# Flamingo block with gated experts and a modulated MLP: two Q/K buffers, six projection products a head, weights split on GpSimd, first up product over six heads

## The chip, the cores and the metric

The kernel runs on one core of one Trainium2 chip. The metric is the device time of one execution in microseconds (us). Three runs of the kernel before took 1077.31, 1077.67 and 1080.08 us; their median is 1077.67 us.

The engines are called by the profile's short names: PE is TensorE (matmuls and transposes), DVE is VectorE, ACT is ScalarE, POOL is GpSimd, SP is SyncE, which here only issues DMAs.

## The reference, cut to what matters

There are 4 batches of 512 tokens with 512 features. First comes a layer norm and an expert layer, in which each token uses one of four experts. Then, on the layer-normed result, a transformer block whose attention output is used only through a 16-wide factor:

```
x1 = x + tanh(g_xattn) * expert_layer(layernorm(x))
y  = layernorm(x1)
h1 = rmsnorm(y) * ln1_w ;  h = rmsnorm(y) * ln2_w
q, k, v = h1 @ Wq.T, h1 @ Wk.T, h1 @ Wv.T          # 16 heads of 32
probs = softmax(causal(q k^T / sqrt(32)))          # per head
attn  = (probs @ v) @ Wo.T
mod   = 0.1 * tanh(attn @ A)                       # 16 wide
gate  = silu(h @ W_in.T + mod * (h @ A) @ B)       # 2048 wide
up    = h @ W_up.T
out   = x1 + tanh(g_ffn) * (y + (gate * up) @ W_down.T)
```

All of it is float32. The kernel gets this precision by writing each operand of a matmul as a high part (rounded by a copy) and a low part (the rest, found by a subtraction), and by three matmuls in the place of one: high times high, low times high, high times low. So a product with a contraction over 512 features is 4 x 3 = 12 matmuls ("12 products"); half of it is 6.

## The kernel before, in words

The expert layer is worked off in 19 items of 128 token rows (the first 160 us of the trace). Then follow the four batches, one after the other; each has a short prelude, the attention over 16 heads, and the MLP in 16 chunks of 128 hidden features. Each engine runs its own instruction stream in order; a semaphore wait in a stream holds up everything behind it in that stream.

The 16 heads of a batch are four quads (`q` = 0 to 3) of four heads (`j` = 0 to 3). Q and K of a quad are one 128-row tile each: the product of the projection weights `wqs` and the transposed rows `hT`, in PSUM bank `QKB` (3). ACT copies the product into its high part (`split_qk`), DVE subtracts to get the low part (`qk_low`, the helper line L1326), and SP copies each head's 32 rows into the buffer `stack` (L307). `qk` holds one quad.

The heads are pipelined. In the step of head n (`head_step`), each engine does this, in this order:

- PE: part of a projection product if the step has one (L510); the transposes of head n+1's probabilities (`turn_probs`, L709; 10 of them), the first of which waits for the first low part of head n, since it overwrites the bank that this is read from; the scores of head n+3 (`scores`, L681 and L685); the product with the values of head n (`attend`, L722; 8 matmuls), which waits for all three low parts of head n.
- ACT: the exponentials of head n+1 (L962) and part of their scaling (L969); `split_qk` where the step has one; the three high parts of head n's turned probabilities (L878).
- DVE: reciprocals and scaling for head n+1 (L1343, L1347); `qk_low` where the step has one; the four row maxima of head n+2 (`maxima`, L1338); the three low parts of head n's turned probabilities (L1326).
- POOL: its part of the scaling (L485), and the low part of a later quad's projection weights (L474).

In the kernel before, K of quad q+1 is projected whole (12 products) at the start of the step j=0 of quad q, and Q of quad q+2 in halves at the start of j=2 and j=3; quads 2 and 3 have less or none of it. ACT's `split_qk` and DVE's `qk_low` take Q of quad q+1 in the step j=0 of quad q, and K of quad q+1 in j=1. So each of them comes one step after the step in which PE finished the product. The high part of the weights is one ACT copy per quad after j=1. Quads 0 and 1 are a hardware loop.

The last quad fills the steps with the first chunk's up product: 3, 3 and 6 products in j = 0, 1, 2 (`up_part`, L769).

The prelude projects Q and K of quad 0 (banks 6 and 7) and Q of quad 1, makes the values (banks 4 and 7), turns the first probabilities, and then clears bank 7 (`ATT`) by a matmul with zeros before the first step.

Of the kernel before, what the change touches and what calls it, by code (L numbers as in the profile page):

```python
# [12 lines left out]
P = 128  # L13
# [27 lines left out]
FIRST_QK = (6, 7)  # L41
VALUES, LOW_RANK = (4, 7), 5
# [12 lines left out]
NORM_AT = 4  # L55

# [3 lines left out]
def build(nc, x, ids, wexp, wov, amat, bmat, ln, gates, wqk, wmlp, out):  # L60
    ctx = ExitStack()
    with ctx:
# [31 lines left out]
        qk = carve(6144, 2048).rearrange("p (m t) -> p m t", m=4)  # L94
        pts = carve(8192, 4 * PACKED).rearrange("p (h a c) -> p h a c", h=2, a=2)
        VS = QH * 64 + 64
        vst = carve(8192 + 4 * PACKED, TT * VS).rearrange("p (t c) -> p t c", t=TT)
        vst_v = vst[:, :, 0:QH * 64].rearrange("p t (h c) -> p t h c", h=QH)
# [155 lines left out]
        def _(sp):  # L254
# [39 lines left out]
            def load_stack(b, q, j):  # L294
                g = b * NQ + q
                if j == 0:


                    sp.wait_ge(qk_lo, g * 2 + 2)
                elif type(q) is int and j == 1:  # L300
                    pass
                else:

                    sp.wait_ge(s_done, g * (3 * QH) + (j - 1) * 3)
                rows = slice(HD * j, HD * j + HD)
                for k, (a, c) in enumerate(((Q_HI, K_HI), (Q_LO, K_HI), (Q_HI, K_LO))):
                    sp.dma_start(stack[HD * k:HD * k + HD, j % 2, :, :].bitcast(F32),  # L307
                                 qk[rows, a:c + 1:c - a, :].bitcast(F32)).then_inc(stk[j % 2], 16)
# [33 lines left out]
            def batch(b, more, first=False):  # L342
                for j in range(2):
                    load_stack(b, 0, j)
                if not first:
                    store_before(b)
                for j in range(2, QH):
                    load_stack(b, 0, j)
                if not first:
                    load_residual(b)  # L350
                with sp.Fori(1, NQ) as q:
# [38 lines left out]
        def _(pool):  # L390
# [26 lines left out]

            def gather(i):
# [47 lines left out]
            for i in range(5 + DT, ITEMS):  # L466
                turn(i)
                if i == ITEMS - 4:
                    pool.wait_ge(wq_hi, 1)
                    g.tensor_tensor(wqs[:, LO, :, :, :], wqk_v[:, :, :, 0:P], wqs[:, HI, :, :, :].bitcast(F32),  # L470
                                    ALU.subtract).then_inc(wq_lo, 1)

            def low(dst, src, high, done):
                g.tensor_tensor(dst, src, high.bitcast(F32), ALU.subtract).then_inc(done, 1)  # L474

            def weights_low(b, q):
                src = wqk_v[:, :, :, bass.ds(q * P, P)]
                pool.wait_ge(wq_hi, b * NQ + q + 1)
                low(wqs[:, LO, :, :, :], src, wqs[:, HI, :, :, :], wq_lo)
# [7 lines left out]
            for b in range(NB):  # L487

                weights_low(b, 1)
                normalise(b * H)  # L490
                for q in range(NQ):
                    for j in range(QH):
                        if q < NQ - 1 or j < QH - 1:
                            normalise((b * NQ + q) * QH + j + 1)
                        if j == 1 and q < NQ - 2:
                            weights_low(b, q + 2)
                if b < NB - 1:

                    weights_low(b + 1, 0)
# [3 lines left out]
        def _(pe):  # L503
# [149 lines left out]
            def project(b, q, which, to=QKB, half=None):  # L653
# [44 lines left out]
            def turn_probs(n, par, first=False):  # L698
# [27 lines left out]
            def head_step(b, q, j, ahead):  # L726
# [12 lines left out]
                if not ahead and j < QH - 1:  # L739
                    if j == 0:  # L740
# [4 lines left out]
                    up_part(0, ((0,), (1,), (2, 3))[j])  # L745
                if ahead or j < QH - 3:
# [18 lines left out]
            def up_part(par, tiles):  # L765

                for k in tiles:
                    for i, (pl, pr) in enumerate(PARTS):
                        mm = pe.matmul(bank[UP[par]][:, :], wch[:, par, pl, (DT + k) * P:(DT + k) * P + P],  # L769
                                       hT[:, pr, k, :], start=k == 0 and i == 0, stop=k == DT - 1 and i == len(PARTS) - 1,  # L770
                                       skip_group_check=True)
                if DT - 1 in tiles:
# [28 lines left out]
            def batch(b, more):  # L801
# [7 lines left out]
                for k in range(DT):  # L809
                    for part in (HI, LO):  # L810
# [3 lines left out]
                values((0, 1))  # L814

# [8 lines left out]
                turn_probs(b * H, 0, first=True)  # L824
                scores(b * H + 2, 0, b * (H // 2) * 48 + 96)

                pe.wait_ge(vpb_ok, b + 1)
                pe.matmul(bank[ATT][:, :], zeror[:, :], hT[:, HI, 0, :], start=True, stop=False,
                          skip_group_check=True).then_inc(pv_done, 1)
                with pe.Fori(0, NQ - 2) as q:  # L830
                    for j in range(QH):
                        head_step(b, q, j, 2)
                for q, ahead in ((NQ - 2, 1), (NQ - 1, 0)):
                    for j in range(QH):
                        head_step(b, q, j, ahead)
# [38 lines left out]
        def _(act):  # L874
# [68 lines left out]
            def split_wqk(b, q):  # L943

                copy(wqs[:, HI, :, :, :], wqk_v[:, :, :, bass.ds(q * P, P)]).then_inc(wq_hi, 1)

            def split_qk(b, q, which, first=False, at=QKB):
                n = b * NQ + q
                act.wait_ge(qk_done, n * 2 + which + 1)
                if which == 0 and not first:  # L950

                    for k in range(2):
                        act.wait_ge(stk[k], n * 96)
                copy(qk[:, (Q_HI, K_HI)[which], :], bank[at][:, :]).then_inc(qk_hi, 1)
# [16 lines left out]
            def head_step(b, q, j, ahead):  # L971
                n = (b * NQ + q) * QH + j
                if ahead or j < QH - 1:
# [8 lines left out]
                if j == 0:  # L982
# [5 lines left out]
                    copy(vst_v[:, :, :, 0:R], vp[:, :, bass.ds(q * QH, QH), :]).then_inc(vst_hi, 1)  # L988

            def quad(b, q, ahead):  # L990
                for j in range(QH):
                    head_step(b, q, j, ahead)
                    if j == 1 and ahead == 2:
                        split_wqk(b, q + 2)
# [36 lines left out]
            def batch(b, more):  # L1031
                split_qk(b, 0, 0, True, FIRST_QK[0])
                split_gate_up(b, 0, 0)
                split_qk(b, 0, 1, True, FIRST_QK[1])
# [15 lines left out]
                with act.Fori(0, NQ - 2) as q:  # L1050
                    quad(b, q, 2)
                quad(b, NQ - 2, 1)
                for j in range(QH):
                    head_step(b, NQ - 1, j, 0)
# [82 lines left out]
        def _(dve):  # L1137
# [190 lines left out]
            def qk_low(b, q, which, at=QKB):  # L1328
                dve.wait_ge(qk_hi, (b * NQ + q) * 2 + which + 1)
                low(qk[:, (Q_LO, K_LO)[which], :], bank[at][:, :], qk[:, (Q_HI, K_HI)[which], :], qk_lo)  # L1330
# [18 lines left out]
            def head_step(b, q, j, ahead):  # L1349

                one_more, two_more = ahead or j < QH - 1, ahead or j < QH - 2
# [3 lines left out]
                if j < 2 and ahead:  # L1355
                    qk_low(b, q + 1, j)
# [5 lines left out]
                if j == 0:  # L1362
                    dve.wait_ge(vst_hi, b * NQ + q + 1)
                    low(vst_v[:, :, :, 32:32 + R], vp[:, :, bass.ds(q * QH, QH), :], vst_v[:, :, :, 0:R], vst_lo)

            def quad(b, q, ahead):


                for j in range(QH):
                    head_step(b, q, j, ahead)  # L1370
# [90 lines left out]
            def batch(b, more):  # L1461
# [7 lines left out]
                normalise(b * H, 0)  # L1469
                maxima(b * H + 1)  # L1470
# [3 lines left out]
                with dve.Fori(0, NQ - 2) as q:  # L1474
                    quad(b, q, 2)
                quad(b, NQ - 2, 1)
                quad(b, NQ - 1, 0)
# [161 lines left out]
```

## Time and profile before

| | |
|---|---|
| median of three runs | 1077.67 us |
| profiled execution, time | 1080.39 us |
| profiled execution, span | 1078.7 us |
| mean granted TensorE clock | 0.997 of 2.4 GHz |
| PE busy | 1035.0 us (96%) |
| DVE busy | 735.5 us (68%) |
| ACT busy | 613.1 us (57%) |
| POOL busy | 177.7 us (16%) |
| steps and prelude of batch 1 | 390.6 to 485.1 us of the span |
| its MLP | 485.1 to about 619 us |

The profile comes from one execution. The profiled execution is 2.7 us above the median of the three runs. Busy time on PE is modelled with the matmuls' drains, so neighbouring matmuls overlap; the distance from one start to the next is what an instruction costs its stream. The views used below are the page itself, the busy time by stretch, the waits, the timeline of one engine (start, duration, engine, line, what it writes and reads, and in brackets the idle time ahead of it with what ended it), and the chain that ended last.

### The profile page before, as it was taken

The numbers are of one execution on the slowest core, as the hardware profiler recorded it, in microseconds if no ns is written. First come the engines' busy times: TensorE is split into PE (matmuls) and PEld (weight loads), VectorE is DVE, ScalarE is ACT, GpSimd is POOL, SyncE is SP. The second block draws the span as 40 slices with busy tenths as digits, with TensorE's granted clock in tenths as the row PEclk, the third lists the DMA queues.
The fourth block names the chain that finished last, engine by engine and source line by source line (L and its number), as shares of the span: only waits on it lengthen the run. The fifth ranks groups of instructions, "written<-read, shape, count | busy, mean of one in ns | idle before, by whom it ended". The sixth has DMA issues, their size and how long they took to land.

```text
span 1078.7 us, 17949 instructions
## 1 busy us (share of the span) xinstructions
PE 1035.0 (96%) x5336; PEld 860.9 (80%) x5337; DVE 735.5 (68%) x1662; ACT 613.1 (57%) x1463; POOL 177.7 (16%) x156
## 2 busy tenths in 40 slices
PE   6999999999999999989999999999999999899998
PEld 6787878777888888878888888778888877788887
DVE  7766747996665559985664589966655689854443
ACT  4464547886444458875444378864354588754342
POOL 4536122320000003320000024200000133200000
PEclk9899999999999999999999999999999999999999
DMA  6534132443322425243322354432234342333221
GB/s 244 188 141 165 39 118 70 97 100 120 105 88 90 151 69 140 64 119 128 108 89 88 108 142 97 112 117 88 88 102 141 85 121 68 79 91 105 88 88 49
DMA packets 47063, 115.59 MB, mean 107 GB/s; under 512 B 6800, under 2 KB 6800, under 8 KB 46096
## 3 DMA queue, kind: packets, MB, share of 16 engines
q1 hardware_dynamic: 43968, 105.06, 33.1%
q0 software_dynamic: 3040, 9.96, 2.7%
q14 instruction: 40, 0.33, 0.1%
q8 instruction: 15, 0.25, 0.1%
HBM read 76.46 MB, written 13.37 MB: 83 GB/s over the span
## 4 chain that ended last, share of the span: by engine, by line
PE 80%; DVE 9%; issue 3%; DMA 3%; ACT 2%; SPq 1%; POOL 1%; DVEq 0%; ACTq 0%; POOLq 0%
PE bank L510 64%; PE bank L709 4%; PE bank L722 3%; DVE wr L1326 3%; DVE nb L1338 3%; PE bank L681 3%; DMA stack<-wr 2%; PE bank L758 1%; SPq L307 1%; DVE big L1347 1%; PE bank L685 1%; ACT big L962 1%; PE bank L769 1%; PE bank L566 1%; DMA big<-in_x,gidx 1%
## 5 line engine op out<-in xcount | busy, mean ns | idle before, releaser
L510 PE MATMUL bank<-hT,wr 128*128 128x512 f32 x1488 | 358.4, 390 | 0.0
L510 PEld LDWEIGHTS bank<-hT,wr 128*128 128x128 f32 x1488 | 278.9, 188 | 59.9 <-issue 1.3
L510 PE MATMUL bank<-wr,actr 128*128 128x512 f32 (+1 forms) x1224 | 303.3, 397 | 2.2 <-DVE actr L1308 1.5
L510 PEld LDWEIGHTS bank<-wr,actr 128*128 128x128 f32 x1224 | 229.1, 190 | 51.1 <-issue 3.3
L1376 DVE SCALAR_TENSOR_TENSOR wr<-stream,lns,wr 128x256 fp32r<-128x256 f32 x256 | 122.3, 538 | 51.0 <-ACT wr L1001 51.0
L1326 DVE TENSOR_TENSOR wr<-bank,wr 128x512 fp32r<-128x512 f32 (+1 forms) x224 | 124.6, 600 | 19.7 <-ACT wr L878 19.7
L962 ACT ACTIVATE big<-bank,nb 128x512 f32<-128x512 f32 (+3 forms) x256 | 131.7, 531 | 9.7 <-DVE nb L1338 8.2
L878 ACT ACTIVATE actr<-act_sb 128x512 fp32r<-128x512 f32 x64 | 40.4, 632 | 145.7 <-DVE act_sb L1390 145.7
L878 ACT ACTIVATE wr<-bank 128x512 fp32r<-128x512 f32 (+1 forms) x224 | 102.6, 532 | 27.8 <-PE bank L510 18.7
L1013 ACT ACTIVATE sil<-bank 128x512 f32<-128x512 f32 x64 | 38.1, 596 | 137.6 <-PE bank L758 137.6
L485 POOL TENSOR_SCALAR big<-big,rr 128x256 f32<-128x256 f32 x64 | 78.0, 1219 | 205.9 <-DVE rr L1343 205.9
L474 POOL TENSOR_TENSOR wqs<-wstage,wqs 128x1024 fp32r<-128x1024 f32 x15 | 36.2, 2410 | 453.4 <-ACT wqs L878 453.4
L1001 ACT ACTIVATE wr<-stream,lns 128x256 fp32r<-128x256 f32 x256 | 108.4, 494 | 0.0
L1338 DVE TENSOR_REDUCE nb<-bank 128x1 f32<-128x512 f32 (+3 forms) x256 | 107.0, 476 | 1.3 <-PE bank L685 1.0
L709 PE MATMUL bank<-ident,big 128*128 128x128 f32 x640 | 86.0, 277 | 22.2 <-DVE wr L1326 22.2
L709 PEld LDWEIGHTS bank<-ident,big 128*128 128x128 f32 x640 | 70.6, 140 | 34.6 <-DVE wr L1326 25.6
L510 PE MATMUL bank<-hT,wqs 128*128 128x512 f32 x384 | 96.3, 398 | 0.9 <-DVE wr L1326 0.9
L1326 DVE TENSOR_TENSOR wr<-stream,wr 128x512 fp32r<-128x512 f32 x64 | 43.8, 690 | 72.4 <-ACT wr L878 71.7
L722 PE MATMUL bank<-wr 128*64 128x512 f32 (+3 forms) x512 | 84.2, 307 | 0.0
L1390 DVE TENSOR_TENSOR act_sb<-bank,sil 128x512 f32<-128x512 f32 x64 | 44.2, 691 | 58.3 <-PE bank L510 51.5
L510 PEld LDWEIGHTS bank<-hT,wqs 128*128 128x128 f32 x384 | 69.7, 188 | 15.8 <-DVE wr L1326 2.2
L722 PEld LDWEIGHTS bank<-wr 128*64 128x64 f32 x512 | 62.0, 134 | 18.8
(182 smaller groups left out, 1078.6 us busy)
## 6 DMA issues: line engine op xcount, KB each, us to landing
stream<-in_wmlp SPq DMA_DIRECT2D x64, 512.0 KB, 4.0
stack<-wr SPq DMA_DIRECT2D x192, 128.0 KB, 2.3
stream<-in_wmlp SPq DMA_DIRECT2D x64, 256.0 KB, 2.7
big<-in_x SPq DMA_DIRECT2D x4, 1024.0 KB, 5.5
big<-y_rows SPq DMA_DIRECT2D x4, 1024.0 KB, 5.6
residual<-big SPq DMA_DIRECT2D x4, 1024.0 KB, 5.1
big<-residual SPq DMA_DIRECT2D x4, 1024.0 KB, 5.6
out<-big SPq DMA_DIRECT2D x3, 1024.0 KB, 4.5
```

What stands on the lines that cost most here:

```text
L485: g.tensor_scalar(rows, rows, rr[:, n % 2, qt:qt + 1], None, ALU.mult).then_inc(pn_pool, 1)
L510: mm = pe.matmul(dst, lhs(pl, k), rhs(pr, k), start=start and i == 0, stop=stop and i == n - 1, skip_group_check=skip)
L709: mm = pe.transpose(bank[bk][:, col + (qt - kt) * P:col + (qt - kt) * P + P], prob[par][:, src:src + P], ident[:, :])
L722: mm = pe.matmul(bank[ATT][0:64, kt * P:S], vst[:, kt, 64 * j:64 * j + 64], pts[:, j % 2, part, at:at + w], start=False, stop=False, skip_ ...
L878: return a.activation(dst, src, ACT.Copy)
L962: a.activation(prob[par][:, at:at + w], bank[bk][:, col:col + w], ACT.Exp, bias=nb[:, qt:qt + 1], accum_out=rs[:, par, qt:qt + 1]).then_in ...
L1001: ins = a.activation(dst[:, :, dt, :], raw[:, :, dt, :], ACT.Copy, scale=lns[:, 1, dt:dt + 1])
L1013: a.activation(sil[:, :], bank[GATE[par]][:, :], ACT.Silu).then_inc(g_silu, 1)
L1326: v.tensor_tensor(dst, src, high.bitcast(F32), ALU.subtract).then_inc(done, 1)
L1338: v.reduce_max(nb[:, qt:qt + 1], bank[bk][:, col:col + P * (qt + 1)], AXX, negate=True).then_inc(nb_ok, 1)
L1376: ins = v.scalar_tensor_tensor(out=dst[:, :, dt, :], in0=raw[:, :, dt, :], scalar=lns[:, 1, dt:dt + 1], in1=high[:, :, dt, :].bitcast(F32) ...
L1390: v.tensor_tensor(act_sb[:, :], bank[UP[par]][:, :], sil[:, :], ALU.mult).then_inc(gu_ok, 1)
```

## The change

What it does:

- `qk` has two buffers, one for even and one for odd quads. ACT waits for `stack` loads of the quad two before instead of the one before.
- PE's projections are in halves of 6 products: K of quad 1 half in the prelude and half at the start of step 0; then one half at the start of every step of quads 0 and 1 (K of q+1 second half in j=0; Q of q+2 in j=1 and j=2; K of q+2 first half in j=3); in quad 2 only j=0 has one.
- ACT's `split_qk` and DVE's `qk_low` take K of quad q+1 in j=0 and Q of quad q+2 in j=2. Q of quad 1 is taken in the prelude.
- The high part of the projection weights of quads 2 and 3 moves from ACT to POOL, and the weights are split for Q and K apart.
- The first up product goes in 6 parts of 2 products into the steps of heads 9 to 14.
- K of quad 0 uses bank 3, the second half of the values bank 6, and the clearing of bank 7 comes before the first scores; the wait for the values' copy moves into `turn_probs`, ahead of its last two transposes.
- The loops over quads are written out; `vst` loses 64 unused columns.

```diff
-FIRST_QK = (6, 7)
-VALUES, LOW_RANK = (4, 7), 5
+FIRST_QK = (6, 3)
+VALUES, LOW_RANK = (4, 6), 5
+UP_PARTS = 6
+UP_FROM = H - 1 - UP_PARTS
@@ GpSimd
+            def weights_high(b, q, which):
+                pool.wait_ge(qk_done, (b * NQ + q - 1) * 2 + which + 1)
+                g.tensor_copy(wqs[:, HI, which, :, :], wqk_v[:, which, :, q * P:q * P + P]).then_inc(wq_hi, 1)
...
-                        if j == 1 and q < NQ - 2:
-                            weights_low(b, q + 2)
+                        if j < 2 and q < NQ - 2:
+                            weights_high(b, q + 2, j)
+                            weights_low(b, q + 2, j)
@@ TensorE: project, turn_probs, head_step
-                    pe.wait_ge(wq_hi, n + 1)
-                    pe.wait_ge(wq_lo, n + 1)
-                    if which and to == QKB:
-                        pe.wait_ge(qk_lo, n * 2 + 1)
+                    pe.wait_ge(wq_lo, n * 2 + which + 1)
+                    if q:
+                        pe.wait_ge(qk_lo, n * 2 + which)
...
+                    elif first and kt == 2:
+                        pe.wait_ge(vpb_ok, values_out)
...
-                if j == 2 and ahead == 2:
-                    project(b, q + 2, 0, half=0)
-                if j == 0 and ahead:
-                    project(b, q + 1, 1)
-                if j == 3 and ahead == 2:
-                    project(b, q + 2, 0, half=1)
-                if ahead or j < QH - 1:
+                if j == 0 and q < NQ - 1:
+                    project(b, q + 1, 1, half=1)
+                elif j and q < NQ - 2:
+                    project(b, q + 2, (0, 0, 1)[j - 1], half=(0, 1, 0)[j - 1])
+                if head < H - 1:
                     turn_probs(n + 1, (j + 1) % 2)
...
-                    up_part(0, ((0,), (1,), (2, 3))[j])
+                    up_part(0, head - UP_FROM)
@@ TensorE: batch
-                with pe.Fori(0, NQ - 2) as q:
+                project(b, 1, 1, half=0)
+                for q in range(NQ):
...
@@ ScalarE head_step
-                if j < 2 and ahead:
-                    split_qk(b, q + 1, j)
+                if j == 0 and q < NQ - 1:
+                    split_qk(b, q + 1, 1)
+                elif j == 2 and q < NQ - 2:
+                    split_qk(b, q + 2, 0)
@@ VectorE head_step
                 if one_more:
                     normalise(n + 1, (j + 1) % 2)
-                if j < 2 and ahead:
-                    qk_low(b, q + 1, j)
+                if j == 0 and q < NQ - 1:
+                    qk_low(b, q + 1, 1)
+                elif j == 2 and q < NQ - 2:
+                    qk_low(b, q + 2, 0)
                 if two_more:
                     maxima(n + 2)
```

## Rows read from the trace of the kernel before

**Rows 1.** The page: busy time of each engine, and TensorE's granted clock in 40 slices.

```profile
PE 1035.0 (96%) x5336; PEld 860.9 (80%) x5337; DVE 735.5 (68%) x1662; ACT 613.1 (57%) x1463; POOL 177.7 (16%) x156
PEclk9899999999999999999999999999999999999999
```

**Rows 2.** Busy time by stretch: batch 0's MLP, batch 1's heads (clock, DMA share, GB/s last).

```profile
256.00:390.00 134.00, 134.00 (x601) 110.52 (x600) 74.60 (x161) 58.82 (x116) 2.54 (x1) 1.00 0.33 107
410.00:486.00 76.00, 70.14 (x455) 58.09 (x454) 70.52 (x161) 63.74 (x190) 22.93 (x17) 1.00 0.39 102
```

**Rows 3.** Waits of PE, whole span: total us, times, longest.

```profile
PE bank L709 <- DVE wr L1326: 22.2, 28, 1.2
```

**Rows 4.** Timeline of PE: a step with a half projection, batch 1.

```profile
447.35 1.60 PE L510 MATMUL bank<-hT,wqs 128*128 128x512 f32 x6
448.79 1.25 PE L709 MATMUL bank<-ident,big 128*128 128x128 f32 x10
449.80 0.47 PE L681 MATMUL bank<-stack 96*128 96x512 f32 x1
...
450.82 1.33 PE L722 MATMUL bank<-wr 128*64 128x512 f32 x8
451.99 3.00 PE L510 MATMUL bank<-hT,wqs 128*128 128x512 f32 x12
```

**Rows 5.** Timeline of PE, batch 1: transposes that open each step's work, and the end.

```profile
408.90 1.25 PE L709 MATMUL bank<-ident,big 128*128 128x128 f32 x10
...
414.47 1.26 PE L709 MATMUL bank<-ident,big 128*128 128x128 f32 x10
...
458.79 1.47 PE L709 MATMUL bank<-ident,big 128*128 128x128 f32 x10 [0.59 <-DVE wr L1326]
...
463.23 1.47 PE L709 MATMUL bank<-ident,big 128*128 128x128 f32 x10 [0.55 <-DVE wr L1326]
464.45 0.48 PE L681 MATMUL bank<-stack 96*128 96x512 f32 x1
...
467.50 1.47 PE L709 MATMUL bank<-ident,big 128*128 128x128 f32 x10 [0.69 <-DVE wr L1326]
...
477.09 1.47 PE L709 MATMUL bank<-ident,big 128*128 128x128 f32 x10 [1.06 <-DVE wr L1326]
...
485.06 5.69 PE L510 MATMUL bank<-hT,wr 128*128 128x512 f32 x24
```

**Rows 6.** Timeline of DVE, batch 1: the values' low part, and one whole step.

```profile
454.38 0.41 DVE L1326 TENSOR_TENSOR wr<-big,wr 128x256 fp32r<-128x256 f32 x1
...
464.02 0.16 DVE L1343 RECIPROCAL rr<-rs 128x4 f32<-128x4 f32 x1
464.22 1.04 DVE L1347 TENSOR_SCALAR big<-big,rr 128x512 f32<-128x512 f32 x2
465.18 1.67 DVE L1338 TENSOR_REDUCE nb<-bank 128x1 f32<-128x512 f32 x4
466.77 1.60 DVE L1326 TENSOR_TENSOR wr<-bank,wr 128x512 fp32r<-128x512 f32 x3
```

**Rows 7.** Chain that ended last, batch 1's prelude: product, high part, low part of K.

```profile
387.96 8.22 PE bank L510 x36
396.20 0.61 ACT wr L878
396.83 0.70 DVE wr L1326
```

**Rows 8.** Groups by line, shapes apart: POOL's weight splits.

```profile
L474 POOL TENSOR_TENSOR wqs<-wstage,wqs 128x1024 fp32r<-128x1024 f32 x15 | 36.2, 2410 | 453.4 <-ACT wqs L878 453.4
```

**Rows 9.** Busy time by stretch, early in the expert stage.

```profile
30.00:40.00 10.00, 8.02 (x30) 6.08 (x30) 7.61 (x21) 3.19 (x5) 5.99 (x9) 0.73 0.79 249
40.00:50.00 10.00, 10.00 (x48) 8.23 (x47) 7.65 (x24) 5.88 (x8) 3.58 (x4) 0.92 0.16 52
```

**Rows 10.** Timeline of PE: one product of 12 in that stretch.

```profile
37.24 4.97 PE L510 MATMUL bank<-wr,actr 128*128 128x512 f32 x12 [0.34 <-DVE actr L1299]
```

More of the change, by code:

```diff
@@ L299, in load_stack @@
                     sp.wait_ge(qk_lo, g * 2 + 2)
[L300 removed]
+                elif q == 0 and j == 1:
                     pass
@@ L350, in batch @@
                     load_residual(b)
-                with sp.Fori(1, NQ) as q:
+                for q in range(1, NQ):
                     for j in range(QH):
@@ L468, in _ @@
                 if i == ITEMS - 4:
[L469 to L479, printed above, removed]
+                    for which in range(2):
+                        weights_low(0, 0, which)
             def normalise(n):
@@ L487, in _ @@
             for b in range(NB):
-                weights_low(b, 1)
+                for which in range(2):
+                    weights_low(b, 1, which)
                 normalise(b * H)
@@ L744, in head_step @@
                         pe.wait_ge(cg_lo, b * NCH + 1)
-                    up_part(0, ((0,), (1,), (2, 3))[j])
-                if ahead or j < QH - 3:
+                    up_part(0, head - UP_FROM)
+                if head < H - 3:
                     m = b * (H // 2) + q * 2 + (j + 3) // 2
@@ L763, in up_product, with up_part @@
                               lambda p, k: hT[:, p, k, :], DT).then_inc(u_done, 1)
[L765 to L772, printed above, removed]
+            def up_part(par, part):
+                n = DT * len(PARTS) // UP_PARTS
+                for i in range(part * n, part * n + n):
+                    k, (pl, pr) = i // len(PARTS), PARTS[i % len(PARTS)]
+                    mm = pe.matmul(bank[UP[par]][:, :], wch[:, par, pl, (DT + k) * P:(DT + k) * P + P],
+                                   hT[:, pr, k, :], start=i == 0, stop=i == DT * len(PARTS) - 1,
+                                   skip_group_check=True)
+                if part == UP_PARTS - 1:
                     mm.then_inc(u_done, 1)
@@ L814, in batch @@
                 values((0, 1))
+                pe.matmul(bank[ATT][:, :], zeror[:, :], hT[:, HI, 0, :], start=True, stop=False,
+                          skip_group_check=True).then_inc(pv_done, 1)
                 pe.wait_ge(qk_lo, b * (NQ * 2) + 2)
@@ L823, in batch @@
                 pe.wait_ge(ha_ok, b + 1)
-                turn_probs(b * H, 0, first=True)
+                turn_probs(b * H, 0, first=True, values_out=b + 1)
                 scores(b * H + 2, 0, b * (H // 2) * 48 + 96)
-                pe.wait_ge(vpb_ok, b + 1)
-                pe.matmul(bank[ATT][:, :], zeror[:, :], hT[:, HI, 0, :], start=True, stop=False,
-                          skip_group_check=True).then_inc(pv_done, 1)
-                with pe.Fori(0, NQ - 2) as q:
+                project(b, 1, 1, half=0)
+                for q in range(NQ):
                     for j in range(QH):
[L832 to L835, printed above, removed]
+                        head_step(b, q, j)
                 pe.wait_ge(exp_ok, (b + 1) * H * 4)
@@ L943, in split_wqk, with split_qk @@
             def split_wqk(b, q):
-                copy(wqs[:, HI, :, :, :], wqk_v[:, :, :, bass.ds(q * P, P)]).then_inc(wq_hi, 1)
-            def split_qk(b, q, which, first=False, at=QKB):
+                for which in range(2):
+                    copy(wqs[:, HI, which, :, :], wqk_v[:, which, :, q * P:q * P + P]).then_inc(wq_hi, 1)
+            def split_qk(b, q, which, at=QKB):
                 n = b * NQ + q
                 act.wait_ge(qk_done, n * 2 + which + 1)
-                if which == 0 and not first:
+                if which == 0 and q >= 2:
                     for k in range(2):
-                        act.wait_ge(stk[k], n * 96)
-                copy(qk[:, (Q_HI, K_HI)[which], :], bank[at][:, :]).then_inc(qk_hi, 1)
+                        act.wait_ge(stk[k], (n - 1) * 96)
+                copy(qk[:, q % 2, (Q_HI, K_HI)[which], :], bank[at][:, :]).then_inc(qk_hi, 1)
             def exponentials(n, par):
@@ L987, in head_step @@
                     act.wait_ge(vst_zero, 1)
[L988 to L994, printed above, removed]
+                    copy(vst_v[:, :, :, 0:R], vp[:, :, q * QH:q * QH + QH, :]).then_inc(vst_hi, 1)
             def split_gate_up(b, c, par):
@@ L1049, in batch @@
                 normalise(b * H, 0)
[L1050 to L1054, printed above, removed]
+                split_qk(b, 1, 0)
+                for q in range(NQ):
+                    for j in range(QH):
+                        head_step(b, q, j)
                 for par in range(2):
@@ L1363, in head_step @@
                     dve.wait_ge(vst_hi, b * NQ + q + 1)
[L1364 to L1370, printed above, removed]
+                    low(vst_v[:, :, :, 32:32 + R], vp[:, :, q * QH:q * QH + QH, :], vst_v[:, :, :, 0:R], vst_lo)
             def gate_up_low(b, c, par):
@@ L1469, in batch @@
                 normalise(b * H, 0)
+                qk_low(b, 1, 0)
                 maxima(b * H + 1)
@@ L1473, in batch @@
                               bank[VALUES[1]][:, :]).then_inc(vpb_ok, 1)
[L1474 to L1477, printed above, removed]
+                for q in range(NQ):
+                    for j in range(QH):
+                        head_step(b, q, j)
                 for par in range(2):
```

42 lines of the change are left out of this document (24 added, 18 removed).

## The prediction

> **What bounds the kernel now.** I read the page first. PE is busy 96% of the span, DVE 68%, and the granted clock stands at nine tenths or more in every slice [rows 1]. So PE is where time is, but a share over the whole span does not say what a stage is worth, so the busy time by stretch came next. In the MLP of a batch PE is busy 134.00 of 134.00 us; nothing of this change touches that stage, and only less PE work could shorten it. In the heads of a batch PE is busy 70.14 of 76.00 us and DVE 70.52 of 76.00 [rows 2]: two engines are both nearly full and hand work to each other. The waits say which hand-over ends late: PE's transposes wait for DVE's low parts, 22.2 us in 28 waits, the longest 1.2 us [rows 3]. That is the whole prize: some 5.5 us a batch.
>
> The timelines show how a step is made up. PE, when it never waits: half a projection 1.44 us (447.35 to 448.79), transposes 1.01, scores 1.02, product with the values 1.17 (450.82 to 451.99), 4.64 us together [rows 4]. Without the projection it is 3.20, and then PE waits: from one step to the next there are 4.27 us (463.23 to 467.50), and the transposes after a wait take 1.22 us to the next start rather than 1.01 [rows 5]. DVE's step is the same 4.27: reciprocal and scaling 1.16 (464.02 to 465.18), maxima 1.59 (to 466.77), low parts 1.53 busy of which the first ends just ahead of the transposes at 467.50, 0.73 us after the low parts began [rows 5, 6]. So steps with half a projection are bound by PE (4.64) and empty ones by DVE (4.27), and spreading the projections evenly looks right. What counts is what DVE's queue waits for in each step.
>
> **The change part by part.**
>
> *The new hand-over.* In the changed code the half that completes a product stands at the start of a step (j=0 for K, j=2 for Q), and in this same step ACT's high part and DVE's low part of it stand ahead of work that PE needs at once. DVE's order is scaling, `qk_low`, maxima, low parts of head n. PE's next instruction after the half projection is the transposes of head n+1, whose first waits for the first low part of head n. Before, the product was a step old when DVE came to it; now it isn't finished when DVE arrives. PE therefore finishes the half, and stands still until ACT and DVE have gone through everything between. Queued behind DVE's wait are the four maxima and the three low parts, behind ACT's the three high parts; PE waits for both.
>
> The price, from rows: start of the half to its last result 1.60 us (the six matmuls' busy time) [rows 4]; ACT starts at 396.20, 0.02 after the product's end at 387.96 + 8.22, and DVE 0.63 after that; the low part 0.70, of which 0.1 overlaps the next, so 0.60 [rows 7]; maxima 1.59 [rows 6]; first low part and hand-over 0.73 [rows 5, 6]. Sum 1.60 + 0.02 + 0.63 + 0.60 + 1.59 + 0.73 = 5.17 us from the start of the half to the transposes, where it was 1.44 without a wait. PE stands idle for 3.57 us of it.
> This comes in j=0 of quads 0, 1, 2 and j=2 of quads 0, 1: 5 times a batch, 20 in all. The bounds of one: below, 3.2 us idle, if DVE's pieces follow each other as closely as in [rows 6] and the hand-overs cost nothing; above, 4.0, by 0.1 more at each of four hand-overs.
>
> *Period of the steps.* With such a hand-over: 1.01 + 1.02 + 1.17 + 5.17 = 8.37 us (transposes to transposes; the ones that open it did not wait) [rows 4]. The step after it has an ordinary half, and its opening transposes did wait: 1.22 + 1.02 + 1.17 + 1.44 = 4.85 [rows 4, 5]. DVE needs 4.27, in j=0 another 0.34 for the values' low part (0.41 less overlap) [rows 6], so 4.61: hidden under PE's 4.85.
>
> *One batch*, in the times of batch 1, by the start of the transposes of head n, T(n). T(0) = 408.90 stays [rows 5]. Then PE does 1.01 + 1.02 + 1.44, and up to 0.5 us for the values' copy, which the last two transposes now wait for (eight transposes and DVE's copy both begin when the values end); I take 0.3. The completing half starts at 412.67, T(1) = 412.67 + 5.17 = 417.84, against 414.47. The zeros' matmul no longer stands there; it falls in PE's wait for the first `stack` load.
> T(9) = 417.84 + 4 x (8.37 + 4.85) = 470.72. The step to T(10) is DVE's, 4.27 + 0.34, so 475.33, against 458.79: 16.5 us late.
> T(10) to T(14) was 18.30 [rows 5]. Now an up part of two products (1.44 / 3 = 0.48 us) stands between transposes and scores in each of four steps, where before one of three products did. Behind the scores stand DVE's maxima; DVE has some 0.3 us of slack there, so each of two steps gives 0.15, and in the quad's first step, where the exponentials are late anyhow, 0.48: in all 18.30 + 0.8 = 19.1. T(14) = 494.4.
> From T(14) to the MLP it was 7.97 [rows 5], all PE or nearly. Four products (0.96 us) less stand there now: 7.0. The MLP begins at 501.4, against 485.06: 16.4 us later, of which the five idle spells are 17.9, their slower restart 1.0, and the evened steps give some 2.5 back.
>
> *POOL's new work.* The low part of 1024 columns takes 2.41 us [rows 8], for half of them some 1.2. The high copy on POOL isn't in the trace; it lies between nothing and 2.41, I take 1.2, as a subtraction of the same size. It is needed by a half projection at least a step later, after 8.37 us, with POOL busy 22.93 of 76 us in this stage [rows 2]. It costs nothing; without that cover it would be up to 2.4 us per quad. ACT gets its copy's time back, but ACT isn't what PE waits for.
>
> *The second buffer, the banks, the written-out loops.* ACT's wait for `stack` loads is behind PE's idle spells: nothing. The splits in the expert stage and in the MLP lie beside a PE that is busy all the time: nothing. For written-out loops I take nothing, within 1 us a batch either way.
>
> *Sum.* 4 x 16.4 = 65.6 us on the profiled execution's 1080.39 gives 1146. The median of the runs is 2.7 us lower: 1077.67 + 65.6 = 1143.3. The bounds: 20 spells by -0.4 and +0.4 give 8 either way, the rest 4: **1131 to 1156**, at an unchanged clock.
>
> **The rivals.**
>
> *The clock falls in the spells.* PE idles 3.6 us in each 13.2 us of the first nine steps; no wait of the transposes before is longer than 1.2 [rows 3]. Early in the expert stage there is a fall to the lower level, 1.2 GHz: a mean of 0.73 over 10 us and 0.92 over the next is 5.4 and 1.6 us at half clock, 7.0 together [rows 9], after short bursts with gaps between. In it 12 products with their restart took 4.97 us [rows 10], against 3.00 at 2.4 GHz [rows 4]. If each spell brought such a fall, 7.0 us would do the work of 4.2, so 2.8 us more each, 20 x 2.8 = 56: 1143 + 56 = 1199. If a third did, 1162. For it: the spells are three times as long as any there now. Against: between two of them lie 9.6 us of dense work. The Trainium skill, "TensorE: Matmul & The Clock Gate", section "HAM oscillation — how this bites in real kernels", warns of just such waits of a few microseconds between bursts, after which every burst starts slow. By that rule this rival's 1199 would be the time; no row here has a spell this long in a dense stretch.
>
> *Shorter spells.* PE's half ends earlier for DVE than its modelled busy end says, and the hand-overs overlap more than in the rows: at half of the maxima's time, 0.8 us a spell, 20 x 0.8 less, 1127. Against it: the hand-overs of [rows 7] are the same kinds of instructions.
>
> *Faster.* The completed products are always there when DVE comes, as before. Then the eight steps from T(1) to T(9) take PE's 4.64, with DVE at 4.27 and at most 0.6 + 0.34 more in a step: 37.1 to 38 us, the next 4.6; T(10) comes at 414.1 + 42.4 = 456.5, 2.3 us earlier, the end 2.5 earlier: 10 in all, 1068. It holds if PE runs at least one step ahead of DVE. Against it: PE cannot, since its transposes wait for the low part that stands behind `qk_low` in DVE's queue. If a second quad's work were taken from a product a step old, this would decide; in the diff it is not.
>
> *The change does nothing*, if the program were bound elsewhere in these steps: PE and DVE are both over 92% busy there [rows 2], so a wait added to both must show.
>
> **How the numbers follow.** Forecast (spells at full clock) 0.72; clock falls 0.16; shorter spells 0.06; faster 0.04; nothing 0.02. Predicted 1143 us. Below 1124 lie the last two and some of the shorter spells; above 1185 lies the half of the clock's rival with a fall in nearly every spell. So 1124 to 1185. A difference under 0.3% (3 us) can't be told from none. Faster 0.04, same 0.02, slower 0.94.
>
> **What would show it.** On PE five waits of some 3.6 us a batch ahead of L709's transposes, ended by DVE's low parts, 20 in all and some 71 us together; on DVE a wait of about 3 us for ACT's high part of K or Q, on ACT one for PE's product, in steps 0, 2, 4, 6, 8; steps alternating between 8.4 and 4.9 us; the clock's row still at 9. The first up product in six pieces, with no wait over 1 us. The MLP stays at its time to the microsecond. It is wrong if the waits are there but the clock's row is lower, or if the steps come out even at 4.6 to 4.9 us with no wait for the product.

## The result and the profile after

The changed kernel takes 1184.73 us (median of 4 runs, 1183.39 to 1185.4) against 1078.88 us of the kernel before in the same session: ratio 1.098, 95% interval 1.0956 to 1.1002. The profiled execution took 1183.39 us, its span 1181.3. The page after, its first rows and the granted clock ([rows 1] before):

```profile
PE 1074.6 (91%) x5336; PEld 892.5 (76%) x5337; DVE 738.6 (63%) x1662; ACT 609.7 (52%) x1463; POOL 191.4 (16%) x188
PEclk9999998899999998899999998899999988899999
```

PE has 40 us more busy time for the same 5336 instructions, so some ran slower, and the clock's row dips four times: once in each batch's heads. The busy time by stretch says the same (heads of batch 1, then its MLP and the first 5 us of the next prelude; after the us of each engine come clock, DMA share and GB/s; [rows 2] before). The MLP keeps a clock of 1.00 and its length; the 0.8 us without work in its row are two gaps ahead of the next batch's first products:

```profile
420.00:540.00 120.00, 98.07 (x565) 82.44 (x564) 85.36 (x188) 75.96 (x221) 29.75 (x26) 0.90 0.36 98
540.00:675.00 135.00, 134.18 (x596) 109.99 (x596) 75.99 (x164) 57.35 (x117) 2.89 (x2) 1.00 0.30 93
```

The wait of the transposes for DVE, 22.2 us before [rows 3], is now

```profile
PE bank L715 <- DVE wr L1324: 86.9, 39, 4.0
```

and PE's timeline shows what a batch looks like (batch 1, only the transposes that open each step's work, [rows 5] before; the product between is shown once):

```profile
441.99 2.14 PE L715 MATMUL bank<-ident,big 128*128 128x128 f32 x10 [3.60 <-DVE wr L1324]
...
448.32 1.25 PE L715 MATMUL bank<-ident,big 128*128 128x128 f32 x10
...
451.52 1.61 PE L515 MATMUL bank<-hT,wqs 128*128 128x512 f32 x6
457.17 2.39 PE L715 MATMUL bank<-ident,big 128*128 128x128 f32 x10 [4.03 <-DVE wr L1324]
...
464.51 1.25 PE L715 MATMUL bank<-ident,big 128*128 128x128 f32 x10
...
472.93 2.25 PE L715 MATMUL bank<-ident,big 128*128 128x128 f32 x10 [3.60 <-DVE wr L1324]
```

A spell every second step, 3.6 to 4.0 us long, where 3.57 was forecast. DVE at the second of them ([rows 6] before):

```profile
454.23 0.69 DVE L1324 TENSOR_TENSOR wr<-bank,wr 128x512 fp32r<-128x512 f32 x1 [4.92 <-ACT wr L880]
454.84 1.67 DVE L1336 TENSOR_REDUCE nb<-bank 128x1 f32<-128x512 f32 x4
456.43 1.61 DVE L1324 TENSOR_TENSOR wr<-bank,wr 128x512 fp32r<-128x512 f32 x3
```

At 454.23 DVE has idled 4.92 us for ACT's high part of Q. It then runs low part, maxima, first low part in the order in which they are queued, and PE's transposes start at 457.17, 0.74 us after the low parts began.

What the forecast left out is in the same transposes: 2.14 to 2.39 us for what takes 1.47 after a wait [rows 5]. The busy time of PE by the microsecond (PE busy, clock, DMA share, GB/s), from the spell on:

```profile
455.00:456.00 1.00, 0.00 (x0) 1.00 0.00 0
456.00:457.00 1.00, 0.00 (x0) 0.53 0.00 0
457.00:458.00 1.00, 0.83 (x4) 0.50 0.00 0
...
461.00:462.00 1.00, 1.00 (x5) 0.50 0.00 0
462.00:463.00 1.00, 1.00 (x6) 0.55 0.55 127
463.00:464.00 1.00, 1.00 (x7) 1.00 0.77 180
```

In this spell the clock falls to 1.2 GHz (0.50) while PE idles and comes back after 5.7 us of work; transposes, scores and the product with the values take 5.90 us (457.17 to 463.07) where they took 3.4. This is one of the dearer falls. Behind the batch's first spell PE starts again at 441.99; the clock falls some 0.4 us after that and is back within 4 us:

```profile
442.00:443.00 1.00, 1.00 (x6) 0.71 0.79 182
...
445.00:446.00 1.00, 1.00 (x7) 0.59 0.00 0
```

Gone through by the microsecond, the whole trace shows a fall at 19 of the 20 spells. The one without, at 188 us, was 3.60 us long like others that had one. The low stretches of the 19 come to 95.5 us, 5.0 us each on average.

### The profile page after: what moved, and what is told of

The parts are those of the page before. It is cut to its first block, busy times and chain, and to the rows that moved or that the text cites. A ratio compares the mean times of both kernels' runs of the same rounds, so it can differ in the third digit from the quotient of the medians.

```text
span 1181.3 us, 17663 instructions
## 1 busy us (share of the span) xinstructions
PE 1074.6 (91%) x5336; PEld 892.5 (76%) x5337; DVE 738.6 (63%) x1662; ACT 609.7 (52%) x1463; POOL 191.4 (16%) x188
## 4 chain that ended last, share of the span: by engine, by line
PE 82%; DVE 8%; issue 3%; ACT 3%; DMA 2%; SPq 1%; DVEq 0%; POOL 0%; ACTq 0%; POOLq 0%
PE bank L515 60%; PE bank L715 8%; PE bank L728 5%; PE bank L684 4%; DVE nb L1336 4%; DVE wr L1324 3%; DMA stack<-wr 2%; PE bank L688 2%; ACT wr L880 2%; PE bank L763 1%; PE bank L571 1%; SPq L309 1%; PE bank L586 1%; PE bank L775 1%; ACT big L965 1%
## 5 line engine op out<-in xcount | busy, mean ns | idle before, releaser
L715 PE MATMUL bank<-ident,big 128*128 128x128 f32 x640 | 104.9, 318 | 86.9 <-DVE wr L1324 86.9
L715 PEld LDWEIGHTS bank<-ident,big 128*128 128x128 f32 x640 | 85.0, 162 | 104.7 <-DVE wr L1324 77.0
L427 POOL TENSOR_TENSOR wqs<-wstage,wqs 128x512 fp32r<-128x512 f32 x32 | 42.7, 1346 | 437.2 <-ACT wqs L880 435.8
L728 PE MATMUL bank<-wr 128*64 128x512 f32 (+3 forms) x512 | 92.5, 326 | 0.3
L728 PEld LDWEIGHTS bank<-wr 128*64 128x64 f32 x512 | 67.6, 146 | 22.4 <-issue 3.9
L684 PE MATMUL bank<-stack 96*128 96x512 f32 (+3 forms) x256 | 83.1, 393 | 1.0 <-DMA stack<-wr 0.5
```

The lines of the kernel that those rows point to most:

```text
L427: g.tensor_tensor(wqs[:, LO, which, :, :], wqk_v[:, which, :, q * P:q * P + P], wqs[:, HI, which, :, :].bitcast(F32), ALU.subtract).then_i ...
L684: pe.matmul(bank[bk][:, col:col + w], stack[:, par, 0, qt * P:qt * P + P], stack[:, par, 1, 0:w], start=start, stop=False, skip_group_chec ...
L715: mm = pe.transpose(bank[bk][:, col + (qt - kt) * P:col + (qt - kt) * P + P], prob[par][:, src:src + P], ident[:, :])
L728: mm = pe.matmul(bank[ATT][0:64, kt * P:S], vst[:, kt, 64 * j:64 * j + 64], pts[:, j % 2, part, at:at + w], start=False, stop=False, skip_ ...
```

## The experiments

Twelve kernels ran, each beside the kernel before on the same chip; ratios are to it. The texts put on record ahead of each run call the explanations by letters. Theory A: PE stands still behind the product's own low part, and the clock falls because PE stands still.

**e1: the parts at the end of the step.** In ACT and DVE the call moves behind the loop over the three parts of head n:

```diff
 DVE head_step (ACT likewise with split_qk, copy)
-                if j == 0 and q < NQ - 1:
-                    qk_low(b, q + 1, 1)
-                elif j == 2 and q < NQ - 2:
-                    qk_low(b, q + 2, 0)
...
                     low(pts[:, j % 2, LO, at:at + w], ...)
+                if j == 0 and q < NQ - 1:
+                    qk_low(b, q + 1, 1)
+                elif j == 2 and q < NQ - 2:
+                    qk_low(b, q + 2, 0)
```

> Changed kernel, but in the steps that complete a product ACT makes its high part after the three high parts of head n, and DVE its low part after the three low parts of head n, instead of ahead of them. Product positions on PE, both Q/K buffers, POOL's splits and the six up parts stay. Theory A (PE stands still because its transposes wait behind the product's own low part, and the clock falls from that): the 20 waits of 3.6 to 4.0 us vanish, no wait over 1.5 us is left, granted clock back to 0.99 or more, steps 1 to 8 of a batch 37 to 38 us, time about 1070. Rival B (POOL's splits, the two buffers or the longer program cost the time): the waits stay and the time stays above 1120. Rival C (the low part is now too late for the stack load of the next quad): waits of PE's scores for the DMA of about 1 us, three a batch, time about 1082.

Measured: 1127.64 us (1.0449, 1.0431 to 1.0466), mean clock 0.977, a fall at 14 of the 20 products. The waits for the low parts went (longest 1.1 us), but another took their place:

```profile
PE bank L684 <- ACT big L965: 37.6, 20, 2.0
PE bank L715 <- DVE wr L1324: 13.2, 18, 1.1
```

Twenty waits again, one a product. ACT now waits for the product at the end of its step, and queued behind that are the next head's exponentials, for which PE's scores wait since they overwrite the bank. ACT's timeline shows the queue:

```profile
424.53 0.60 ACT L880 ACTIVATE wr<-bank 128x512 fp32r<-128x512 f32 x1 [2.35 <-PE bank L515]
425.03 0.41 ACT L880 ACTIVATE wr<-big 128x256 fp32r<-128x256 f32 x1
425.33 0.68 ACT L965 ACTIVATE big<-bank,nb 128x512 f32<-128x512 f32 x1
```

Neither A, which saw no second queue and said 1070, nor B or C foretold this. The DVE part of the chain is confirmed; ACT's part had been overlooked.

**e2: maxima first.** One exchange on DVE, ACT as it was:

```diff
-                if j == 0 and q < NQ - 1:
-                    qk_low(b, q + 1, 1)
-                elif j == 2 and q < NQ - 2:
-                    qk_low(b, q + 2, 0)
                 if two_more:
                     maxima(n + 2)
+                if j == 0 and q < NQ - 1:
+                    qk_low(b, q + 1, 1)
+                elif j == 2 and q < NQ - 2:
+                    qk_low(b, q + 2, 0)
```

> Changed kernel, with one pair of DVE calls exchanged: the four maxima of head n+2 before the product's low part instead of behind it. ACT and PE unchanged. Theory A: the maxima (1.59 us) leave the chain from product to transposes, so each of the 20 waits goes from 3.6 to 2.0 us. With the clock no longer falling: 32 us for the waits and some 35 us for the clock, 1118. With the clock falling as before: about 1153. Rival (the wait is not this chain): no change, 1185.

Measured: 1159.16 us (1.075, 1.0709 to 1.0791), clock 0.966. The spells fell by the maxima's time, to 2.01 to 2.44 us:

```profile
PE bank L715 <- DVE wr L1324: 54.9, 38, 2.4
PE bank L684 <- ACT big L965: 6.8, 12, 0.9
```

86.9 - 54.9 = 32.0 us off the transposes' waits, the 32 forecast; 6.8 came back as waits for exponentials. The case with a falling clock (1153) is the nearer one: the clock fell at 14 of the 20 spells, though each was only 2.0 to 2.4 us long.

**e3: the spells filled.** Fourteen matmuls with zero weights where PE stood still:

```diff
                 elif j and q < NQ - 2:
                     project(b, q + 2, (0, 0, 1)[j - 1], half=(0, 1, 0)[j - 1])
+                if (j == 0 and q < NQ - 1) or (j == 2 and q < NQ - 2):
+                    for _ in range(14):
+                        pe.matmul(bank[ATT][:, :], zeror[:, :], hT[:, HI, 0, :], start=False, stop=False,
+                                  skip_group_check=True)
```

> Changed kernel with 14 more matmuls (512 columns, zero weights, added into the values' bank, which they leave as it is) on PE right behind each half that completes a product, where PE now stands idle; nothing else is changed. They take 14 x 0.22 = 3.1 us of the 3.6. Theory A (the chain sets the step, and the clock's part of the loss comes from PE being idle): the step's length by the chain stays, the clock stays at 2.4 GHz, and the time falls by the clock's part alone, some 35 to 40 us, to about 1147, although PE does 280 more matmuls. Rival D (the slow matmuls behind the waits have another cause than idle time): clock row as low as before and time 1185 or more. Rival E (PE is the bound): 62 us more, 1245.

Measured: 1150.37 us (1.0668, 1.065 to 1.0686), clock 0.999. PE does 280 matmuls more, 3.3 us a spell, and the kernel is 34.4 us faster:

```profile
431.65 3.33 PE L744 MATMUL bank<-hT,zeror 128*128 128x512 f32 x14
435.41 1.47 PE L715 MATMUL bank<-ident,big 128*128 128x128 f32 x10 [0.43 <-DVE wr L1328]
```

The transposes are back at 1.47 us, and still the last thing that they wait for is DVE's low part, so the fill did not lengthen the chain. The clock's part is thus 34.4 us, 1.7 a spell; PE as the bound (E) and another cause for the slow matmuls (D) fall.

**e4: the places of before.** All of the change but the steps of products and parts:

```diff
-                if j == 0 and q < NQ - 1:
-                    project(b, q + 1, 1, half=1)
-                elif j and q < NQ - 2:
-                    project(b, q + 2, (0, 0, 1)[j - 1], half=(0, 1, 0)[j - 1])
+                if j == 2 and q < NQ - 2:
+                    project(b, q + 2, 0, half=0)
+                if j == 0 and q < NQ - 1:
+                    project(b, q + 1, 1)
+                if j == 3 and q < NQ - 2:
+                    project(b, q + 2, 0, half=1)
... DVE (ACT likewise with split_qk)
-                if j == 0 and q < NQ - 1:
-                    qk_low(b, q + 1, 1)
-                elif j == 2 and q < NQ - 2:
-                    qk_low(b, q + 2, 0)
+                if j < 2 and q < NQ - 1:
+                    qk_low(b, q + 1, j)
```

> Changed kernel with the projections and their high and low parts put back where they were (K of the next quad whole in j=0, Q of the quad after in halves in j=2 and j=3; parts in j=0 and j=1, one step after the product), in PE, ACT and DVE. Two buffers, POOL's high and low splits, the banks, written-out loops and the six up parts stay. Theory A: those parts cost nearly nothing; 1076 to 1082. Rival B (these parts cost the time): above 1120.

Measured: 1081.21 us (1.0019, 1.0003 to 1.0036). POOL's splits, the second buffer, the banks, the written-out loops and the six up parts together cost about 2 us (0.3 to 3.9 by the interval). Rival B falls.

**e5 and e6: a product a step old, from either side.** e5 moves PE's halves one step earlier (with them POOL's splits, and K of quad 1 is whole in the prelude) and leaves ACT's and DVE's parts; e6 leaves PE and moves the parts.

```diff
 e5, PE
-                if j == 0 and q < NQ - 1:
-                    project(b, q + 1, 1, half=1)
-                elif j and q < NQ - 2:
-                    project(b, q + 2, (0, 0, 1)[j - 1], half=(0, 1, 0)[j - 1])
+                if q < NQ - 2:
+                    project(b, q + 2, j // 2, half=j % 2)
 e6, DVE (ACT likewise with split_qk)
-                if j == 0 and q < NQ - 1:
+                if j == 1 and q < NQ - 1:
                     qk_low(b, q + 1, 1)
-                elif j == 2 and q < NQ - 2:
+                elif j == 3 and q < NQ - 2:
                     qk_low(b, q + 2, 0)
```

> Changed kernel with PE's half projections one step earlier: K of quad 1 whole in the prelude, then Q of quad q+2 in j=0 and j=1 and K of quad q+2 in j=2 and j=3 of quads 0 and 1. ACT's and DVE's parts stay in j=0 and j=2, so each product is a step old when they come, as in the kernel before. POOL splits the weights a step earlier too, and SP's load for a quad's first head also waits for the scores of the head two before. Theory A (a product must be a step old): no wait of PE above 1.2 us, clock 0.99 or more, steps 1 to 7 at 4.65 us, time 1070 to 1082. Rival F (both parts in one step with the maxima overload DVE or ACT, whatever the age of the product): waits of 1 to 2 us stay in the steps 0, 2, 4, 6, 8 and the time above 1110.

> Changed kernel with PE as it is, and ACT's high and DVE's low part of K moved from j=0 to j=1, those of Q from j=2 to j=3, at the same place within the step (after the scaling, ahead of the maxima). The product is then a step old from the other side. Theory A: no wait of 1.8 us or more for exponentials (as the late order within the step had) or low parts. Left over: the scores of the next quad's first head wait for its stack load, since K's low part comes 2.7 us after the transposes and SP and the DMA take 4.1 us more, about 1 us, three times a batch: 1080 to 1090, clock 0.99. Rival F: above 1110.

Measured: e5 1089.73 us (1.0103, 1.0088 to 1.0119), clock 0.998; e6 1079.80 us (1.0009, 1.0 to 1.0019), clock 0.997. Both lose the spells, and the slow clock but for one fall in e6. With six products in each of the first nine steps of e6, PE waits 19.0 us for low parts:

```profile
PE bank L715 <- DVE wr L1324: 19.0, 23, 1.7
```

Of the DMA waits expected for e6, about 1 us three times a batch, next to nothing is there:

```profile
PE bank L684 <- DMA stack<-wr: 1.0, 3, 0.5
```

e5 is 8 us over the top of A's range: its projection of Q of quad 2 now waits in step 0 for DVE to free the bank (row below, 6.0 us in all), and it has eight steps without a projection, where e6 has seven. The rest of e5's excess I haven't traced.

```profile
PE bank L521 <- DVE wr L1328: 6.0, 4, 1.5
```

**e7 and e8: is DVE's load what bounds the empty steps?** One line, in e5's kernel (e7) and in the kernel before (e8):

```diff
-NORM_DVE, NORM_ACT, NORM_POOL = (3, 2), (0,), (1,)
+NORM_DVE, NORM_ACT, NORM_POOL = (3,), (2,), (1, 0)
```

> The kernel with halves one step earlier, and the probabilities' scaling spread anew: DVE scales only the 512 columns of tile 3, ACT tile 2 (384) and POOL tiles 1 and 0 (256 and 128). DVE's step falls from 4.27 to some 3.8 us, ACT's rises by 0.1, POOL's by 0.6. Theory A with DVE as the bound of the empty steps: the seven steps without a projection shorten by some 0.3 each, 8 to 14 us in all below the kernel with halves earlier. Rival G (in the empty steps the chain scores, maxima, low part, transposes is the bound, not DVE's load): under 3 us below it.

> Kernel before, with only the scaling spread anew (DVE tile 3, ACT tile 2, POOL tiles 1 and 0). It has seven steps a batch bound by DVE at 4.27 us and PE needs 3.2 us in them: 4 x 7 x 0.3 to 0.45 = 8 to 13 us less, about 1067. Rival G: within 3 us of the kernel before.

Measured: e7 1087.32 us, 2.4 below e5; e8 1080.07 us (1.0012, 1.0 to 1.0025). DVE's busy time fell by 30 us; e7 gained 2.4 us by it and e8 nothing. Both are inside what rival G gave (under 3 us), and outside the 8 to 14 us of the other case. DVE in an empty step of e8:

```profile
464.78 0.49 DVE L1347 TENSOR_SCALAR big<-big,rr 128x512 f32<-128x512 f32 x1
465.60 1.69 DVE L1338 TENSOR_REDUCE nb<-bank 128x1 f32<-128x512 f32 x4 [0.33 <-PE bank L685]
467.20 1.61 DVE L1326 TENSOR_TENSOR wr<-bank,wr 128x512 fp32r<-128x512 f32 x3
```

It now waits 0.33 us for the scores, and the step is 4.15 us instead of 4.27: the chain transposes, scores, maxima, first low part lies close under DVE's load. That the shorter steps (4.15 us twice, and 4.90 for 5.32 in the last) did not show in the time has a second reason: from T(0) to T(14) batch 1 takes 68.22 us in e8 and 68.19 before, because three earlier steps (from T(0), T(1) and T(9)) came out 0.17 to 0.18 us longer and others a little. No run separates why; ACT and POOL had got 11 and 36 us more work. So the wait for the scores is shown in the empty steps; that this chain is what kept the whole time from falling is argued only.

**e9 to e12: where the up parts stand.** e9 is the kernel before with the change's six parts alone; e10 has them behind the scores; e11 is e6 with them behind the scores; e12 is the kernel before with them behind the product with the values:

```diff
 e12, PE head_step of the kernel before
-                if not ahead and j < QH - 1:
-                    if j == 0:
-                        ...
-                    up_part(0, ((0,), (1,), (2, 3))[j])
...
                 attend(b, q, n, j)
+                if UP_FROM <= head < H - 1:
+                    if head == UP_FROM:
+                        ...
+                    up_part(0, head - UP_FROM)
```

> Kernel before, with one part of the change alone: the first up product in six parts of two products in heads 9 to 14, between transposes and scores, instead of 3, 3 and 6 in heads 12 to 14. Forecast of the prediction: 0.8 us more in the steps to T(14), 1.0 less behind it, so no change (within 2 us). Theory H, from the changed kernel's steps of 4.60 us with an up part against 4.27 without: the maxima wait for scores that come 0.48 us later, so four steps cost 0.33 each, three more than before; with the tail's 1.0 us back, about 0 to 2 us slower in all.

> The same six up parts in the kernel before, but behind the scores of head n+3 instead of ahead of them, where PE waits 0.55 us a step for DVE anyway. Theory H: the steps go back to 4.27 us, the up product is hidden in waits, and the 1.0 us of the tail stays won: 1.3 to 2 us a batch, 5 to 8 us in all below the kernel before, about 1072. Rival I (the waits belong to DVE's load and the tail is bound by it too): within 2 us of the kernel before.

> The changed kernel with K's and Q's parts a step later (j=1 and j=3), and the up parts behind the scores. That kernel with the parts ahead stood at 1079.8. Theory H: 1.3 us a batch off it, about 1074, below the kernel before by 4 us. What is left against the kernel before with the parts behind is about 0.6 us a batch of PE waiting for nothing shown at the head of a batch and in the written-out program.

> The same six up parts in the kernel before, now behind the product with the values of head n, as the last thing of the step. Ahead of that product they held back ACT's copy of the values in the last quad's first step, which waits for the product, and the exponentials queued behind it: 5.84 us from T(13) to T(14) against 5.32 in the kernel before. Theory J: this step goes back to about 5.3, so 0.5 us a batch, 2 us in all below the kernel with the parts behind the scores, about 1075. Rival I (the tail is bound otherwise): within 1 us of it, 1077.

Measured: e9 1079.53 us (1.0003, 0.9994 to 1.0012); e10 1077.24 (0.9979, 0.997 to 0.9989); e11 1077.56 (0.9991, 0.9982 to 1.0); e12 1075.70 against 1079.01 (0.997, 0.9959 to 0.9982). In e9 a step with a part takes 4.60 us, in e10 4.27:

```profile
461.58 1.47 PE L711 MATMUL bank<-ident,big 128*128 128x128 f32 x10 [0.58 <-DVE wr L1330]
462.81 0.70 PE L773 MATMUL bank<-hT,wr 128*128 128x512 f32 x2
...
466.18 1.47 PE L711 MATMUL bank<-ident,big 128*128 128x128 f32 x10 [0.58 <-DVE wr L1330]
```

```profile
462.12 1.48 PE L711 MATMUL bank<-ident,big 128*128 128x128 f32 x10
...
466.39 1.47 PE L711 MATMUL bank<-ident,big 128*128 128x128 f32 x10 [0.18 <-DVE wr L1330]
```

So the place counts in the steps (theory H), though e10's gain is 2 us, not 5 to 8, and e11 came to 1077.56 where 1074 was expected. In the last quad's first step the wait for the exponentials grew; these waits are in e10

```profile
PE bank L683 <- ACT big L966: 3.6, 4, 1.0
```

e12 took that back in this step as theory J said (469.73 to 475.04, 5.31 us, for e10's 5.84). In the whole time e12 and e10 can't be told apart by their intervals. Both are below the kernel before, by 3.3 us (0.3%) and 2.0 us (0.2%), with intervals that leave out no difference; the prediction had called 3 us the limit.

## Why the prediction was right, and where not

- *Direction, place and length of the wait*: right. Five spells a batch, in the steps 0, 2, 4, 6, 8, each ended by DVE's low part behind `qk_low` and the maxima. 3.60 us measured for 3.57 in K's spells; Q's were 3.74 and 4.03 (in the last batch all were 3.69). What adds to Q's I did not try. The profile lays six of ACT's eight waits there to a `stack` load, a semaphore that ACT waits for only with Q, and in the spell shown ACT starts 0.48 us behind the product's end (453.13 to 453.61), with the next K 0.04 (469.33 to 469.37). The prediction had put this wait at nothing.
- *The sum without the clock*: 1143.3 us forecast; e3, the same spells at full clock, 1150.37. Of the 7 us missing 1.2 are the kernel before, whose median is 1078.88 here for 1077.67. The rest is in part the sizes of small terms: Q's spells, up parts at 0.9 us a batch and not 0.8 (T(10) to T(14): 508.88 to 528.12, 19.24 us, for 18.30 before), and gaps of 0.2 to 0.8 us at a batch's first products, which PE shows with the written-out program:

```profile
417.06 3.47 PE L515 MATMUL bank<-hT,wqs 128*128 128x512 f32 x14 [0.69 <-issue]
```

- *The clock*: the term that failed. I put it at nothing in the forecast and gave its fall 0.16, with 9.6 us of dense work between spells as the reason against. The prediction's own sign of being wrong came true: the waits are there and the clock's row is lower. It fell in 19 of 20 spells, at 34.4 us in all: 105.9 us were lost, 65.6 forecast, and a third of the loss is the clock. The measured time is 0.3 us inside the range's upper end, because the range reached toward this rival; that it fell inside is in part luck. The rival's own 1199 was too high, as a spell cost 1.7 us by the clock and not 2.8: the low stretches were 5.0 us long on average for the 7.0 taken, and part of each lay in PE's idle time. The rule of the Trainium skill that I cited ("TensorE: Matmul & The Clock Gate", section "HAM oscillation — how this bites in real kernels"), weighed against the change, was the better guide; the trace agrees with it (19 of 20 spells of 3.6 to 4.0 us).
- *POOL, the second buffer, banks*: forecast at nothing, e4 measures them and the up parts together at 2 us. POOL's high copy takes 0.61 us (1.2 taken) and its low part 1.29.
- *The faster case* asked for a product a step old. e6 gave it that, and the time was 1079.8, not 1068. Its steps show where it failed. T(0) to T(10) takes 49.21 us in batch 1 of e6 (408.42 to 457.63), 49.89 before and 47.6 in the forecast: five steps come at the forecast 4.65 us, but four (from T(2), T(5), T(6) and T(9)) take 5.13 to 5.33. A likely reason, which no run separates, is that DVE in a step with the low part of Q or K needs 4.88 us from one reciprocal to the next, more than PE's 4.64:

```profile
413.98 0.17 DVE L1341 RECIPROCAL rr<-rs 128x4 f32<-128x4 f32 x1
...
418.86 0.16 DVE L1341 RECIPROCAL rr<-rs 128x4 f32<-128x4 f32 x1
```

From T(10) to T(14) e6 takes 20.30 us, for 19.1 forecast and 18.30 before. The two together are 2.8 us a batch, 11 of the 12 us missing.

## What to carry to other kernels

When a producer's piece and the consumer's part of it are put into the same step of a software pipeline, look at what is queued behind the consumer's wait, on each engine that takes part, and whether the producer's next instruction needs that. Here it did, on DVE and, once DVE was mended, on ACT; only a full step between product and use (e5, e6) removed it. Fill work belongs behind the last instruction that another engine's critical work waits for (e12), not ahead of it (e9), even if both orders seem to fill the same wait.

## What the runs showed of the hardware

The clock falls at shorter spells than I expected. In e1 PE's waits in the heads are at most 2.0 us, one for each product, and the mean clock is 0.977; six matmuls take 2.41 us there for 1.60:

```profile
440.39 0.50 PE L684 MATMUL bank<-stack 96*128 96x512 f32 x1 [1.77 <-ACT big L965]
...
443.37 2.41 PE L515 MATMUL bank<-hT,wqs 128*128 128x512 f32 x6
```

With waits up to 1.5 us (e5) there is no fall in the heads (0.998). In e6 a wait of 1.7 us comes once a batch, and one of the four brought a fall, 1.2 us after PE had started again at 457.63:

```profile
458.00:459.00 1.00, 1.00 (x10) 0.90 0.98 225
459.00:460.00 1.00, 1.00 (x5) 0.50 0.76 174
```

So the same wait brings a fall at one time and none at another, as the spell at 188 us of the changed kernel shows too. Matmuls with zero weights kept the clock up here (e3, 0.999), so an idle PE can cost more than the same time spent on useless work: 1184.73 against 1150.37 us.
